# Cross-attention and expert FFN on one core: batch 0's context quantised by columns, two weight halves made by POOL

## The reference

```python
x = x + xattn(layernorm(x), ctx)        # x, ctx: 4 x 512 x 512
x = x + ffn(layernorm(x), ...)
# xattn: both operands in blocks of 128 along K are scaled by their largest
#   absolute value, rounded to float8_e4m3, scaled back; ctx has one scale per 128x128 block
xq, wq = quant_act_1x128(xn), quant_weight_128x128(ctx)
out = einsum('emk,enk->emn', xq, wq)
# ffn, 2048 tokens: softmax router over 128 experts, top 4
gate, up = xt @ w_gate, xt @ w_up       # 8 basis functions of 256
basis = silu(gate) * up
mixed = mix[topk_idx] . basis           # mix from the amplitudes
out = sum_k coeff_k * (mixed_k @ w_down) + shared expert (512 wide)
```

## Time and profile before

| what | us |
|---|---|
| median of 3 runs (lowest, highest) | 595.44 (594.39, 595.62) |
| the profiled execution | 594.92 |
| its span, first to last instruction | 593.1 |
| TensorE busy | 535.1 (90%) |
| VectorE busy | 392.9 (66%) |
| ScalarE busy | 242.5 (41%) |
| POOL busy | 201.9 (34%) |

### The profile page before, as it was taken

The page is one execution under the profiler, slowest core; times in us unless marked ns, Lnnn a source line. Parts: engine busy times, 40 slices in busy tenths (PEclk is TensorE's granted clock), DMA queues, the critical chain, the costliest instruction groups (busy, mean ns, idle before and its releaser), DMA issues.

```text
span 593.1 us, 7851 instructions
## 1 busy us (share of the span) xinstructions
PE 535.1 (90%) x2571; PEld 252.7 (43%) x2586; DVE 392.9 (66%) x1122; ACT 242.5 (41%) x355; POOL 201.9 (34%) x238
## 2 busy tenths in 40 slices
PE   0359979779999999999999999999999999999983
PEld 0124434334544444444444444444444444444431
DVE  6977888788775677768474777776666747463311
ACT  4686884553524242343433332344333343322210
POOL 2431052443714135534414134735132131402020
PEclk9999999999999999999999999999999999999997
DMA  8624432012212312112123121121212212020101
GB/s 299 251 88 141 165 102 28 18 28 59 49 28 70 90 36 55 36 40 50 27 59 102 45 47 27 45 45 36 54 35 43 48 27 64 9 54 10 45 0 44
DMA packets 61752, 37.08 MB, mean 63 GB/s; under 512 B 49168, under 2 KB 49680, under 8 KB 61712
## 3 DMA queue, kind: packets, MB, share of 16 engines
q1 hardware_dynamic: 61712, 36.59, 23.3%
HBM read 20.72 MB, written 4.19 MB: 42 GB/s over the span
## 4 chain that ended last, share of the span: by engine, by line
PE 72%; DVE 9%; issue 3%; ACT 2%; POOL 1%; DMA 0%; POOLq 0%; DVEq 0%; SPq 0%
PE up L982 29%; PE gate L982 29%; PE even L1012 10%; PE odd L964 2%; DVE part L1296 1%; DVE x L1204 1%; PE odd L904 1%; DVE before L1243 1%; DVE gate_up L1367 1%; DVE down_lo L1367 1%; POOL hid L562 0%; DVE ctx_m L1126 0%; PE even L904 0%; DMA hT_hi<-hs_hi 0%; PE up L935 0%
## 5 line engine op out<-in xcount | busy, mean ns | idle before, releaser
L982 PE MATMUL up<-gate_up,zT_hi 128*128 128x512 f16 x600 | 178.5, 379 | 2.8 <-DVE y_out L1334 2.1
L982 PE MATMUL gate<-gate_up,zT_hi 128*128 128x512 f16 x600 | 178.4, 379 | 0.1
L705 ACT ACTIVATE silu<-gate,w_back 128x512 f32<-128x512 f32 x75 | 51.6, 687 | 174.8 <-PE gate L982 173.9
L982 PE MATMUL up<-gate_up,zT_lo 128*128 128x512 f16 x300 | 113.7, 379 | 0.0
L982 PE MATMUL gate<-gate_up,zT_lo 128*128 128x512 f16 x300 | 113.7, 379 | 0.0
L1296 DVE SCALAR_TENSOR_TENSOR part<-up,coef,silu 128x256 f32<-128x256 f32 x128 | 55.9, 479 | 54.7 <-PE up L982 46.2
L562 POOL TENSOR_TENSOR hid<-hid,part 128x256 f32<-128x256 f32 x48 | 34.9, 727 | 152.1 <-DVE part L1296 152.1
L982 PEld LDWEIGHTS gate<-gate_up,zT_hi 128*128 128x128 f16 x600 | 58.5, 100 | 65.7 <-issue 0.6
L982 PEld LDWEIGHTS up<-gate_up,zT_hi 128*128 128x128 f16 x600 | 57.5, 98 | 62.6
L546 POOL TENSOR_TENSOR gain<-var,minus_half 128x1 f32<-128x1 f32 x16 | 11.3, 705 | 131.8 <-DVE neg_mean L1218 131.8
L982 PEld LDWEIGHTS up<-gate_up,zT_lo 128*128 128x128 f16 x300 | 29.3, 98 | 35.4
(11 more groups left out here) (176 smaller groups left out, 793.1 us busy)
## 6 DMA issues: line engine op xcount, KB each, us to landing
ctx_in<-in_ctx SPq DMA_DIRECT2D x16, 256.0 KB, 3.7
x_in<-in_x SPq DMA_DIRECT2D x16, 256.0 KB, 2.9
out<-y_out SPq DMA_DIRECT2D x16, 256.0 KB, 2.2
stage<-in_L_ffn_w_gate SPq DMA_DIRECT2D x2, 1024.0 KB, 7.5
stage<-in_L_ffn_w_up SPq DMA_DIRECT2D x2, 1024.0 KB, 5.0
stage<-in_L_ffn_shared_w_gate SPq DMA_DIRECT2D x1, 1024.0 KB, 7.7
stage<-in_L_ffn_shared_w_up SPq DMA_DIRECT2D x1, 1024.0 KB, 8.8
ctx_qT<-in_L_ffn_w_up SPq DMA_DIRECT2D x1, 1024.0 KB, 12.1
```

Source lines behind the costliest of these rows:

```text
L705: nc.scalar.activation(silu[:, k % 2, :], gate_ps[k % 2][:], ACT.Silu, scale=w_back[:, n:n + 1] if t else 1.0 / LN_GAIN).then_inc(silu_don ...
L982: mm = nc.tensor.matmul(ps[:], zT[a][:, t % 2, kc, :], wgu[:, n - 1 + i, w, kc, :], start=(m == 0), stop=(m == 3 * KC - 1))
```

## The change

Batch 0's context is scaled, masked, rounded and turned by column blocks (`ctx_cols`: 128 columns of all four row blocks) instead of row blocks. ScalarE scales column blocks 0 and 2, POOL 1 and 3; VectorE rounds all four, and x's tile 0 too (`round_x`). `attend(0, kc)` waits for column block kc alone, and `attention(0, kc)` stands between the roundings. `quantise_x` is cut into `measure_x` and `shrink_x`, with `measure_x(0)` ahead of `lane_ctx(0)`. The calls of all five engines up to tile 1 are put in another order: on VectorE `scale_of_w(0)` and `mixes` follow `stats2(0)`, on ScalarE `exps(0)` goes ahead of `silus(0, -1)` and `keep_x(1)`, on TensorE `spread_w(1)` follows `turn_x(1)`. The high halves of chunks 5 and 6 are made by POOL with one `tensor_scalar` each (128x2048), and `lo_w` waits for POOL there. From batch 1 on the context is quantised as before.

```diff
+    ON_POOL = (5, 6)
...
-            out = lane("ctx", 0) + lane("w", 0) + [("x", 0)] + lane("w", 1) + [("x", 1)]
+            out = lane("ctx", 0) + [("x", 0)] + lane("w", 0) + [("flip_w", 1), ("x", 1), ("spread_w", 1)]
             out += lane("w", 2) + lane("w", 3) + [("z", 1)] + lane("w", 4) + lane("w", 5)
...
-            if c in (2, 3):
-                eng.wait_ge(ctx_round_dve, CTX_ROUNDS * (c - 1))
+            if c < NB:
+                eng.wait_ge(ctx_round_dve, CTX_ROUNDS * (c + 1))
             else:
-                eng.wait_ge(ctx_round_pool, CTX_ROUNDS * (c + 1 if c < 2 else c - 1))
+                eng.wait_ge(ctx_round_pool, CTX_ROUNDS * (c - NB + 1))
...
+        def ctx_cols(kc):
+            return ctx_in[:, :, kc * P:(kc + 1) * P]
+        def by_block(a):
+            return a.rearrange("p (c n) -> p c n", c=KC)
...
-                c4 = lambda a: a.rearrange("p (c n) -> p c n", c=KC)
-                nc.gpsimd.tensor_tensor(c4(ctx_in[:, k]), c4(ctx_in[:, k]),
-                                        ctx_mul[:, k].unsqueeze(2).to_broadcast([P, KC, P]), ALU.mult
+                rows, by = (ctx_cols(c), ctx_mul[:, :, c]) if c < NB else (by_block(ctx_in[:, k]), ctx_mul[:, k])
+                nc.gpsimd.tensor_tensor(rows, rows, by.unsqueeze(2).to_broadcast([P, KC, P]), ALU.mult
...
+            def split_w(n):
+                wait_scale(pool, n)
+                nc.gpsimd.tensor_scalar(w_part(0, n), w_staged(n), w_scale[:, n:n + 1], None, ALU.mult
+                                        ).then_inc(w_hi_pool, 1)
...
-            round_ctx(0)
-            round_ctx(1)
-            round_x(0)
+            scale_ctx(1)
+            scale_ctx(3)
             rstd_of(1)
             rstd2_of(0)
             round_x(1)
             rstd_of(2)
+            split_w(5)
             rstd2_of(1)
+            split_w(6)
             mix_parts(0, 0)
...
-                for kc in range(KC):
+                for i in range(KC):
+                    k, kc = (i, c) if c < NB else (c % NB, i)
...
+            scale_ctx(0)
             scale_ctx(2)
             sum_w(0)
+            keep_x(0)
+            keep_ctx(0)
             sum_w(1)
+            keep_ctx(1)
             sum_w(2)
-            keep_ctx(0)
-            scale_ctx(3)
+            keep_ctx(2)
+            keep_ctx(3)
             sum_w(3)
-            keep_ctx(1)
-            keep_ctx(2)
-            keep_x(0)
-            keep_ctx(3)
+            norm2(0)
+            norm1(1)
+            keep_z32()
             split_w(0)
             split_w(1)
-            norm1(1)
             sum_w(4)
-            norm2(0)
+            exps(0)
+            silus(0, -1)
+            keep_x(1)
             split_w(2)
-            keep_z32()
             sum_w(5)
             sum_w(6)
-            silus(0, -1)
-            keep_x(1)
-            exps(0)
             split_w(3)
             sum_w(7)
             split_w(4)
             keep_weight(0)
             abs_shared(0)
-            split_w(5)
             sum_w(8)
             silus(0, 0)
             norm1(2)
             norm2(1)
-            split_w(6)
             split_w(7)
...
-                    pe.wait_ge(kept0, turn_of(HI, "ctx", t // NB * NB + NB - 1) + 1)
+                    if t >= NB:
+                        pe.wait_ge(kept0, turn_of(HI, "ctx", t // NB * NB + NB - 1) + 1)
                     wait_at(pe, down_read, t - 2)
                 elif kc == 1:
                     wait_at(pe, top_step, TOP_STEPS * (t - 1) + 1 if t else 0)
                 else:
                     pe.wait_ge(att_step, ATT_STEPS * t + (kc - 1) * NB)
+                if t < NB:
+                    pe.wait_ge(kept0, turn_of(HI, "ctx", kc) + 1)
...
             spread_ctx(0)
+            turn_x(0)
             turn_ctx(0)
+            turn_ctx(1)
+            attend(0, 0)
+            turn_ctx(2)
+            attend(0, 1)
             flip_w(0)
+            turn_ctx(3)
+            attend(0, 2)
+            attend(0, 3)
+            turn_z32()
             spread_w(0)
-            turn_ctx(1)
-            turn_ctx(2)
-            turn_x(0)
-            turn_ctx(3)
-            for kc in range(KC):
-                attend(0, kc)
-            turn_z32()
             route32()
-            pair32(-1, {1: lambda: flip_w(1), 4: lambda: spread_w(1), 6: lambda: [turn_x(1), attend(1, 0)]})
-            pair32(0, {2: lambda: [attend(1, 1), flip_w(2)], 4: lambda: spread_w(2), 5: lambda: attend(1, 2),
-                       7: lambda: [turn_weight(0), attend(1, 3)]})
-            pair32(1, {2: lambda: coefs(0), 5: lambda: flip_w(3), 7: lambda: spread_w(3)})
-            pair32(2, {5: lambda: [turn_z(1, HI), turn_z(1, LO)]})
+            pair32(-1, {4: lambda: flip_w(1), 6: lambda: turn_x(1)})
+            pair32(0, {0: lambda: spread_w(1), 2: lambda: attend(1, 0), 4: lambda: attend(1, 1), 5: lambda: flip_w(2),
+                       6: lambda: attend(1, 2)})
+            pair32(1, {0: lambda: [turn_weight(0), attend(1, 3)], 1: lambda: spread_w(2), 2: lambda: coefs(0),
+                       6: lambda: flip_w(3)})
+            pair32(2, {1: lambda: spread_w(3), 5: lambda: [turn_z(1, HI), turn_z(1, LO)]})
...
+            def round_x(t):
+                ch = Chain(dve, x_round, X_ROUNDS, t)
+                dve.wait_ge(xq_step, XQ_STEPS * (t + 1))
+                ch.did(nc.vector.tensor_tensor(x_v[:], x_v[:], x_m[:], ALU.add))
+                ch.sync()
+                ch.did(nc.vector.tensor_tensor(x_q[:], x_v[:], x_m[:], ALU.subtract))
...
+            def measure_x(t):
+                ch = Chain(dve, xq_step, XQ_STEPS, t)
+                dve.wait_ge(y_done, 2 * (t + 1))
+                ch.did(nc.vector.tensor_reduce(x_max[:], by_block(y[:]), AX.X, ALU.max, apply_absolute_value=True))
+                ch.sync()
+                ch.did(nc.vector.tensor_scalar(x_scale[:], x_max[:], ACT_EPS, 1.0 / FP8_MAX, ALU.max, ALU.mult))
+                ch.sync()
+                ch.did(nc.vector.reciprocal(x_mul[:], x_scale[:]))
+                return ch
...
-                dve.wait_ge(w_hi_done, ORDER.index(n) + 1)
+                if n in ON_POOL:
+                    dve.wait_ge(w_hi_pool, ON_POOL.index(n) + 1)
+                else:
+                    dve.wait_ge(w_hi_done, [m for m in ORDER if m not in ON_POOL].index(n) + 1)
...
+            x_chain = measure_x(0)
             scales_ctx(lane_ctx(0), 0)
-            scale_ctx(0)
-            scale_ctx(1)
-            mask_ctx(0)
-            mask_ctx(1)
-            quantise_x(0)
-            lane_chain = lane_w(0)
-            mask_ctx(2)
-            round_ctx(2)
-            scales_w(lane_chain, 0)
-            mask_ctx(3)
-            round_ctx(3)
+            shrink_x(x_chain, 0)
+            round_x(0)
+            for kc in range(KC):
+                mask_ctx(kc)
+                round_ctx(kc)
+                if kc >= 2:
+                    attention(0, kc - 2)
+            attention(0, 2)
             stats(1)
+            attention(0, 3)
+            stats2(0)
+            scale_of_w(0)
             mixes()
-            attention(0, 0, 1, 2, 3)
-            stats2(0)
             lo_w(0)
             quantise_x(1)
             lo_w(1)
...
```

More of the change, by code:

```diff
@@ L386, in load_ctx @@
                 if b > 0:
-                    wait_ctx_rounded(sp, c - NB)
+                    wait_ctx_rounded(sp, c - NB if b > 1 else NB - 1)
                 sp.dma_start(ctx_in[:, k, :], ctx_t[c * P:(c + 1) * P, :]).then_inc(ctx_loaded[k], 16)
@@ L403, in load_chunk @@
                 elif SLOT[n] == 4:
-                    for c in (1, 3):
-                        wait_ctx_rounded(sp, c)
+                    wait_ctx_rounded(sp, NB - 1)
                 slot = stage[SLOT[n]]
@@ L514, in round_ctx @@
                 k = c % NB
-                ch = Chain(pool, ctx_round_pool, CTX_ROUNDS, c if c < 2 else c - 2)
+                ch = Chain(pool, ctx_round_pool, CTX_ROUNDS, c - NB)
                 pool.wait_ge(ctx_mask, CTX_MASKS * (c + 1))
@@ L518, in round_ctx @@
                 ch.sync()
-                if c >= 2:
+                if c >= NB:
                     pool.wait_ge(turned0, turn_of(HI, "ctx", c - 2) + 1)
@@ L641, in keep_ctx @@
                     wait_ready(act, DOWN)
-                nc.scalar.copy(ctx_qT[:, b, :, k * P:(k + 1) * P],
-                               turned[0].bitcast(BF16)[:, 0:KC * P].rearrange("p (c n) -> p c n", c=KC)
-                               ).then_inc(kept0, 1)
+                rows = ctx_qT[:, 0, c].rearrange("p (c n) -> p c n", c=KC) if b == 0 else ctx_qT[:, b, :, k * P:(k + 1) * P]
+                nc.scalar.copy(rows, by_block(turned[0].bitcast(BF16)[:, 0:KC * P])).then_inc(kept0, 1)
             def norm1(t):
@@ L1138, in mask_ctx @@
                 else:
-                    dve.wait_ge(ctx_scaled_pool, c - 2 * NB + 1)
+                    dve.wait_ge(ctx_scaled_pool, c - 2 * NB + 3)
                 if c >= 2:
```

(24 more changed lines are left out.)

21 lines of the change are left out of this document (5 added, 16 removed).

## The result

The changed kernel takes 603.16 us (median of 4 runs, 601.5 to 605.53), against 595.53 for the kernel before in the same comparison: a ratio of 1.0134, 95% interval 1.0103 to 1.0165. It is 7.6 us slower; forecast were 2.6. The profiled execution took 603.29 us, its span 601.5. The direction was right and the size lay outside the range.

The account below looks back on a forecast made before the run. The start of tile 1 counts, set by VectorE's list late in the startup. The 2.7 us gain at route32 is outweighed by waits on ScalarE and POOL, tile 1 2.6 late: 595.44 + 2.6 = 598.0 us, range 592.7 to 600.8.

Parts of the forecast that it names:

- What bounds the kernel: TensorE is busy from 150 us on; in the startup's second half VectorE's list sets when tile 1 begins.
- Part 1: Quantising batch 0: stats2(0) ends at 32.3, route32 starts at 36.0 instead of 38.74, a gain of 2.7 us.
- the first term: Start of quantising batch 0: POOL's scalings 2.4, shrink_x 0.8, mask and rounding 2.25, little overlap; x rounded at 16.5.
- Part 2: Work moved behind stats2(0) and route32: scales_w(1) comes 2.2 us late on VectorE, attention(1, 2) 1.7 late.
- the new wait: Before scales_w(1): spread_w(1) waits for keep_x(1), behind exps(0) and silus(0, -1) on ScalarE; scales_w(1) at 48.9, 2.2 late.
- Part 3: High halves of chunks 5 and 6 on POOL, 2.0 us each, hold VectorE; tile 1 comes about 2.6 late.
- my upper bound of 4.79: Longest time taken for a POOL half of 2048 columns, from four two-input scalings of 512 columns.
- the two waits: VectorE held by POOL's halves: lo_w(3) waits 0.8 us, the last step of lane_w(3) 1.3.
- After that the list is the old one: Behind lane_w(3)'s last step nothing more is lost; flip_w(5) and all of tile 1 come about 2.6 late.
- my two signs of being wrong: The forecast is wrong if exps(0) doesn't hold keep_x(1), or if lo_w(7) ends before 79.87.
- The third: POOL's halves take 4.8 us, with two lo_w or lane steps behind them: kernel at 603.6 us; chance 0.08.
- The first, faster: VectorE's waits are absorbed, lo_w(7) ends at 78.6: 594.2 us, 592.7 with all of route32's 2.7 kept; chance 0.27.

Follow-up runs that it names:

- e9_earlier2: The changed kernel with both halves back on ScalarE, keep_x(1) and split_w(2) ahead of silus(0, -1), spread_w(2) earlier, split_w(5) later: 593.67 us, ratio 0.9982.
- e5_spread3: The changed kernel, POOL's halves kept, with spread_w(3) three steps later on TensorE: 600.86 us, ratio 1.0087 against the kernel before.
- e1_act56: The changed kernel with both high halves back on ScalarE at their old places: 595.53 us, ratio 1.0009 against the kernel before.
- e10_two_in: The changed kernel with POOL's halves as a two-input tensor_tensor, the scale spread over the columns: 601.33 us, ratio 1.0111 against the kernel before.
- e6_late6: The changed kernel with POOL's second half started only when scales_w(3) is done: 605.17 us, ratio 1.0161 against the kernel before.
- e3_pieces: The changed kernel with each POOL half in four instructions of 512 columns: 603.85 us, ratio 1.0146 against the kernel before.

## Why the prediction was right and wrong

**What bounds the kernel: right, but for TensorE.** From tile 1 to TensorE's last products it is 496.8 to 496.9 us in all fourteen traces (584.18 less 87.33 in the kernel before), so all is decided ahead of tile 1. From `scales_w(2)` on VectorE's list sets the end as long as TensorE doesn't stand still; `e9_earlier2` turned 0.9 us there (56.34 against 57.28) into 0.9 at tile 1 (85.30 against 86.23).

**Part 1: right, and better than forecast.** `stats2(0)` ended at 31.25 (31.11 + 0.14; forecast 32.3), `route32` started at 34.89 (36.0): a gain of 3.85, not 2.7. The 1.1 that I had too late lie in the first term: x was rounded at 15.39 (14.70 + 0.69), not 16.5, for POOL's two scalings and `shrink_x` started earlier and overlapped more than I allowed. From there to `stats2(0)` it took 15.9 us, as forecast (15.8). VectorE's masks on columns with a stride of 512 took 0.42, as in the earlier trace rows; nothing was the right value.

**Part 2: the mechanism right, its size too large.** The old gap of 3.06 us before `lane_w(1)` is used up (0.22 is left), and the new wait is there: `spread_w(1)` waits for `keep_x(1)` on ScalarE, VectorE 2.60 us behind it. But `flip_w(1)` came at 41.6, not 43.4, so `scales_w(1)` was 0.8 late instead of 2.2, and `attention(1, 2)` 0.3 instead of 1.7. Here the steps of part 1 that I had too late are the reason: `route32` 1.1, and the gate half ahead of the flip 4.9 us long, not 5.6.

**Part 3: the failed step.** "I take 2.0, near the lower end, for there is one input." It was 5.45, above my upper bound of 4.79 too. I chose by the number of inputs, from rows of other operations (a memset below, a `tensor_tensor` above); the runs show that the operation decides: copy 1.89, `tensor_tensor` 3.60, `tensor_scalar` 5.37 to 5.45. The Trainium skill (GPSIMD Engine Reference, Engine selection) calls one-input work roughly line rate: this holds for the copy and not for the `tensor_scalar`. With the copy's row in the place that I forecast, the two waits were 0.6 and 0.8, against my 0.8 and 1.3, and the kernel took 596.67.

**The missing step: TensorE behind the held lane.** "After that the list is the old one": I counted the hold of `lane_w(3)` for VectorE's list alone and put TensorE behind it at nothing. TensorE stood for 7.09 us at `spread_w(3)`, its clock went to 1.2 GHz, and the slow products held silu(0, 1) and the last half: 1.8 + 1.7 us of the 8.2. In `e5_spread3` both are gone. Neither of my two signs of being wrong could show this or the long row: `exps(0)` does hold `keep_x(1)`, and `lo_w(7)` ends at 86.35, behind 79.87.

**The rivals.** The third, POOL at its upper end, gave 603.6 and came at 603.16, which is luck. By my own sum the measured row makes 2.6 + 2 x 3.45 = 9.5, that is 604.9; VectorE was held less than that (2.4 and 2.7 instead of 4.3 and 4.8) and part 2 cost 1.4 less, and TensorE's term, which I did not have, filled most of the gap. The first, faster, would have needed the halves off POOL: with them off it is 595.53, not 594.2. The 3.85 us of `route32` meet VectorE's longer list (its logits came 0.8 earlier in `e1_act56`, 42.77 against 43.58), then the waits for `spread_w(1)` and `spread_w(2)`. `e9_earlier2` shortens those two and reaches the rival's time.

## What to carry to other kernels

In these runs an instruction's duration on POOL went by its operation and not by the number of its inputs: look for a row of the same operation, and where there is none, let the range reach past the dearest row. When a long POOL row is put beside VectorE's list, name every VectorE instruction that will fall into it, down to the smallest, and the TensorE instruction behind that, because TensorE paid again here: its granted clock stood at 0.50 behind the wait. A gain ahead of several engines' lists is worth only what the waits further down give back; move the wait that is the last one on the bounding engine.

## What the runs showed that I had not expected

- POOL's `tensor_scalar` (2.66 ns a column) is slower than its `tensor_tensor` on the same columns (1.76) and its copy (0.92). The three are from one shape, 128x2048, float32 to float16.
- The hold ends at two different times. The Trainium skill (SBUF — State Buffer, Terms) has the shared port pair held for the full instruction. This case agrees for the copy and the `tensor_tensor`: `lo_w(3)` ended 2.15 and 2.14 us after POOL's row (59.32 + 2.92 = 62.24 against 60.09; 63.24 against 61.10). It doesn't for the `tensor_scalar`: `lo_w(3)` ended at 63.48, only 0.42 after POOL's 63.06, so it ran beside the row's last 1.7 us, while the 2x2 step was held to the row's end. `lo_w(4)` shows the same: it starts 3.65 us behind the start of POOL's second row in the change (70.37 less 66.72) and 3.53 in `e10_two_in` (69.98 less 66.45), though the rows are 5.45 and 3.60 long. So the last 1.8 us of the `tensor_scalar` held the 2x2 step and TensorE behind it, but not VectorE's list. Why the two differ was not tried.
- The order of two short instructions can move a run by up to 1.2 us: the last step of `lane_w(1)` is 0.22 long in `e1_act56`, 0.26 in the change, 0.92 in `e6_late6` and 1.20 in `e3_pieces`, by where it falls beside POOL's `round_x(1)`.
- At the kernel's end TensorE waits some 7.5 us for a transpose by DMA, and its last 18 products start at the low clock (0.50 from 584 to 586 us in the kernel before). They took 5.5 to 7.0 us by when the clock came back (584.18 to 589.82 in the kernel before; 588.66 to 595.60 in `e5_spread3`). That is over 1 us between kernels whose edits are 500 us away, and as large as a difference of 0.2%.
